# A graph-attention layer and its feed-forward layer on one core: adjacency cast in the transfer, largest score formed by TensorE, one bias product, normalisation on ScalarE

## The reference, cut to what matters

```
xn  = layernorm(x)
seq = (xn @ W_seq).reshape(2048, 16, 32)
score1, score2 = seq . a1, seq . a2                       # per head
scores = leaky_relu(score1[i] + score2[j], 0.2) + (1 - adj) * -65500
hidden = softmax(scores) @ seq  -> (2048, 512) @ W_out + b_out
x = x + elu(hidden)
xn = layernorm(x)
routed = top-2-of-8 experts (latent 256) on xn;  shared = relu(xn @ up.T)**2 @ down.T
x = x + routed + shared
```

## Time and profile before

| | |
|---|---|
| median of 3 runs | 1060.65 us (1060.53 to 1062.79) |
| profiled execution | 1060.79 us, its span 1058.9 us |
| busy: PE, DVE, ACT, POOL | 95%, 76%, 63%, 24% of the span |
| PE's first product with x; first attention unit | 17.82 us; 99.76 us |
| first to last tile of the output projection | 487.86 to 566.77 us |
| mean granted clock of PE | 0.98 of full |

### The profile page before, as it was taken

How to read it: one execution, slowest core, us unless ns; L and a number is a source line. 1 busy time by engine, 2 the same in 40 slices (tenths; PEclk the granted TensorE clock), 3 DMA queues, 4 the chain that set the end, 5 groups by cost and what they waited for, 6 DMA issues and landing times.

```text
span 1058.9 us, 27195 instructions
## 1 busy us (share of the span) xinstructions
PE 1006.7 (95%) x11256; PEld 890.0 (84%) x11256; DVE 803.9 (76%) x1197; ACT 666.5 (63%) x990; POOL 251.5 (24%) x271
## 2 busy tenths in 40 slices
PE   5996889999999999999899999999999999989998
PEld 4875889999999999997677888888888877778887
DVE  6776899999999999993699433448775668975554
ACT  2668999999989889933356333344454546655431
POOL 1103124334333443363331000000065000006500
PEclk9996999999999999999899999999999999999999
DMA  8781111111111111623635000020063124453242
GB/s 301 249 313 40 41 62 43 45 61 42 43 52 52 42 43 52 225 67 132 229 116 208 1 1 1 1 80 1 26 207 117 50 80 131 130 158 112 85 134 99
DMA packets 53778, 102.45 MB, mean 97 GB/s; under 512 B 6161, under 2 KB 26257, under 8 KB 53138
## 3 DMA queue, kind: packets, MB, share of 16 engines
q1 hardware_dynamic: 47666, 82.83, 23.6%
q0 software_dynamic: 3072, 8.39, 2.5%
q10 hardware_dynamic: 2928, 9.57, 2.4%
HBM read 74.69 MB, written 26.08 MB: 95 GB/s over the span
## 4 chain that ended last, share of the span: by engine, by line
PE 47%; issue 2%; DVE 2%; DMA 1%; POOL 1%; ACT 0%; SPq 0%; POOLq 0%; DVEq 0%; ACTq 0%
PE bank L1758 16%; PE bank L1291 16%; PE bank L668 3%; PE bank L1835 2%; PE bank L1786 1%; PE bank L1787 1%; PE bank L1789 1%; DMA xs<-sorted_latent_rows 1%; PE bank L1805 1%; PE bank L1779 1%; PE bank L1743 1%; PE bank L1741 1%; PE bank L665 1%; PE bank L1740 1%; DVE acc_rest L1492 0%
## 5 line engine op out<-in xcount | busy, mean ns | idle before, releaser
L730 ACT ACTIVATE arena<-arena 128x1024 fp8e4<-128x1024 f32 x320 | 336.6, 1136 | 2.5 <-ACT arena L722 1.6
L956 PE MATMUL bank<-arena 128*128 128x132 f16 x4096 | 285.6, 222 | 19.0 <-DVE arena L816 7.6
L956 PEld LDWEIGHTS bank<-arena 128*128 128x128 fp8e4 x4096 | 246.6, 98 | 20.8 <-issue 8.6
L1291 PE MATMUL bank<-xt,up_parts 128*128 128x512 f32 x768 | 186.2, 391 | 0.0
L1758 PE MATMUL bank<-down_parts,h_parts 128*128 128x512 f32 x768 | 184.5, 389 | 0.1
L960 PE MATMUL bank<-arena 128*128 128x66 f16 x4096 | 173.5, 196 | 0.0
L794 DVE TENSOR_SCALAR arena<-arena 128x1024 uint8<-128x1024 f32 x192 | 167.8, 940 | 2.7 <-DMA arena<-s_rows 2.7
L1758 PEld LDWEIGHTS bank<-down_parts,h_parts 128*128 128x128 f32 x768 | 143.9, 188 | 30.5 <-issue 0.5
L1291 PEld LDWEIGHTS bank<-xt,up_parts 128*128 128x128 f32 x768 | 142.3, 188 | 28.6 <-ACT relu_sb L1240 0.2
L960 PEld LDWEIGHTS bank<-arena 128*128 128x128 fp8e4 x4096 | 154.9, 98 | 0.0
L1265 DVE TENSOR_TENSOR relu_sb<-relu_sb 128x512 f32<-128x512 f32 x64 | 44.4, 693 | 118.0 <-ACT relu_sb L1240 110.9
(11 more groups left out here) (231 smaller groups left out, 1403.9 us busy)
## 6 DMA issues: line engine op xcount, KB each, us to landing
hid<-in_adjT SPq DMA_DIRECT2D x32, 512.0 KB, 5.8
arena<-s_rows SPq DMA_DIRECT2D x30, 512.0 KB, 3.7
sorted_latent_rows<-zeros SPq DMA_DIRECT2D x1, 4992.0 KB, 18.5
xs<-sorted_latent_rows SPq DMA_DIRECT2D x39, 128.0 KB, 2.1
sorted_expert_rows<-expert_y SPq DMA_DIRECT2D x39, 128.0 KB, 1.7
arena<-in_x SPq DMA_DIRECT2D x4, 1024.0 KB, 10.8
xr<-in_x SPq DMA_DIRECT2D x16, 256.0 KB, 2.8
up_sb<-in_upT ACTq DMA_DIRECT2D x1, 4096.0 KB, 14.0
```

Of the source, the lines that this page charges most:

```text
L730: last = nc.scalar.activation(m8[:, k, j, :], s1b[:, k % 2, :], ACT.Sigmoid, bias=bias_now[:, k % 2, j:j + 1], scale=STEEP, saturate=False)
L956: last = nc.tensor.matmul(o, m8[:, k, j, i * P:(i + 1) * P], vs[:, b, j, :], start=(j == 0), stop=(j == T - 1))
L1291: last = nc.tensor.matmul(bank[6 + s % 2][:, :], sa[:, s % 2, a, k, :], xt[c][:, b, k, :], start=(i == 0), stop=(i == len(mm) - 1))
```

## The change

Setup: GpSimd issues eight transfers of 512 adjacency rows by 1024 columns that cast float32 to fp8 on the way (+1; `apply_empty_rows` now sets the sign as well as the empty rows), after tile 2 and 3 of x have landed and ahead of its roots; the 32 casts on DVE and ACT are gone. Weights are loaded, centred (now on ACT) and transposed by quarters; x in groups of 2, 2, 4, 4, 4 tiles. Constants are issued by ACT. The largest score over the partitions is formed by a transpose and a product on PE with a maximum on DVE, in place of a reduction on GpSimd. Score rows are stored by SP, the first two ahead of the others. The values of the first head are made in two parts (12 tiles, 4 tiles), and the first unit starts on the first part; the order of the first units is changed on all engines.

Output projection: the bias as one product with 128 rows instead of two with one; the second layer norm as one ACT instruction with scale and bias, for which GpSimd forms -mean/std in two further steps; up is loaded in four parts, issued after tiles 2, 4, 6 and 8, down after tile 10.

The diff, cut to its core (left out: buffer placements, semaphore names, ACT's order in setup, which loses its casts, and the sign constants):

```diff
...
+        TOP_BANK = bank[4]
+        X_GROUPS = ((0, 2), (2, 4), (4, 8), (8, 12), (12, 16))
+        def x_group(t):
+            return next(g for g, (a, b) in enumerate(X_GROUPS) if a <= t < b)
         def setup_loads(sp):
-            sp.dma_start(ident, ident_in[:, :]).then_inc(consts_loaded, 16)
-            sp.dma_start(a_cols_sb, a_cols[:, :]).then_inc(consts_loaded, 16)
-            sp.dma_start(a_mask_sb.rearrange("p c h -> p (c h)"), a_mask[:, :]).then_inc(consts_loaded, 16)
-            for c in range(2):
-                sp.dma_start(wt_sb[:, 2 * c:2 * c + 2, :], w_seqT[c * 2 * P:(c + 1) * 2 * P, :].rearrange("(c p) k -> p c k", p=P)
-                             ).then_inc(wt_loaded[c], 16)
-            for g in range(4):
-                sp.dma_start(x_sb[:, 4 * g:4 * g + 4, :],
-                             x[512 * g:512 * g + 512, :].rearrange("(t p) d -> p t d", p=P)
-                             ).then_inc(x_loaded[g], 16)
-            for q in range(HALVES):
-                if q >= AB:
-                    sp.wait_ge(cast_by_act if (q - AB) % 2 else cast_by_dve, (q - AB) // 2 + 1)
-                sp.dma_start(adj_in[:, q % AB, :], adjT[(q % T) * P:(q % T + 1) * P, (q // T) * IC:(q // T + 1) * IC]
-                             ).then_inc(adj_loaded[q % AB], 16)
+            for c in range(KD):
+                sp.dma_start(wt_sb[:, c, :], w_seqT[c * P:(c + 1) * P, :]).then_inc(wt_loaded[c], 16)
+            for g, (a, b) in enumerate(X_GROUPS):
+                sp.dma_start(x_sb[:, a // 8, a % 8:a % 8 + b - a, :], x[a * P:b * P, :].rearrange("(t p) d -> p t d", p=P)).then_inc(x_loaded[g], 16)
+            sp.wait_ge(st_copied, 6)
+            sp.dma_start(s1_dram[0:2, 0:IC], s1_rows[0:2, 0:IC]).then_inc(s1_stored, 16)
+            sp.wait_ge(s1_stored, 16)
+            for k in range(2):
+                sp.dma_start(s1b[:, k, :], s1_dram[k:k + 1, 0:IC].to_broadcast([P, IC])).then_inc(s1_staged[k], 16)
+            sp.wait_ge(st_copied, 8)
+            sp.dma_start(s1_dram[2:H, 0:IC], s1_rows[2:H, 0:IC]).then_inc(s1_stored, 16)
+            sp.dma_start(s1_dram[:, IC:], s1_rows[:, IC:]).then_inc(s1_stored, 16)
+            sp.wait_ge(s1_stored, 48)
...
+            def centre_w(c):
+                act.wait_ge(w_mean_ready, c + 1)
+                nc.scalar.activation(wt_sb[:, c, :], wt_sb[:, c, :], ACT.Identity, bias=w_nmean[:, c:c + 1]).then_inc(w_centred, 1)
+            def high_w(c):
+                act.wait_ge(w_in_psum, c + 1)
+                nc.scalar.copy(w_hi[:, :, c * P:(c + 1) * P],
+                               bank[4 + c][:, :].rearrange("p (k n) -> p k n", k=KD)).then_inc(w_high, 1)
...
+            def load_adjacency(half):
+                cols = slice(half * IC, (half + 1) * IC)
+                for g in range(AG):
+                    pool.dma_start(adj8[:, 4 * g:4 * g + 4, cols],
+                                   adjT[512 * g:512 * g + 512, cols].rearrange("(j p) i -> p j i", p=P)
+                                   ).then_inc(adj_loaded[half], 16)
+            pool.wait_ge(x_loaded[1], 16)
+            load_adjacency(0)
+            load_adjacency(1)
+            root(0)
+            root(1)
             largest(0, slice(H, H + 1))
+            root(2)
+            root(3)
...
+            def mean_w(c):
+                dve.wait_ge(wt_loaded[c], 16)
+                step(nc.vector.bn_stats(w_stat6[:, c, :], wt_sb[:, c, :]))
+                step(nc.vector.bn_aggr(w_mv[:, c, :], w_stat6[:, c, :]))
+                nc.vector.tensor_scalar(w_nmean[:, c:c + 1], w_mv[:, c, 0:1], -1.0, None, ALU.mult).then_inc(w_mean_ready, 1)
+            def low_w(c):
+                dve.wait_ge(w_high, c + 1)
+                part = w_hi[:, :, c * P:(c + 1) * P]
+                nc.vector.tensor_tensor(w_lo[:, :, c * P:(c + 1) * P], bank[4 + c][:, :].rearrange("p (k n) -> p k n", k=KD),
+                                        part.bitcast(f32), ALU.subtract).then_inc(w_ready, 1)
...
+                dve.wait_ge(s_in_psum, 2)
+                step(nc.vector.reduce_max(topm[0:H, :], TOP_BANK[0:H, 0:P], AX.X))
+                nc.vector.tensor_scalar(topd[0:H, :], ident[0:H, 0:H], topm[0:H, 0:1], None, ALU.mult).then_inc(tops_ready, 1)
+                dve.wait_ge(s_in_psum, 3)
+                step(nc.vector.tensor_copy(topr[:, 0:H], TOP_BANK[:, P:P + H]))
...
+            bound_v()
+            row_stats(0, 1)
+            for c in range(KD):
+                low_w(c)
             low_x(0, 1)
+            row_stats(2, 3)
+            low_x(2, 3)
+            variances(0)
             stats(1)
-            low_x(2, 3)
             low_wa()
-            cast(0)
+            low_x(4, 5, 6)
             stats(2)
-            low_x(4, 5, 6)
-            cast(2)
+            low_x(7, 8, 9, 10)
             stats(3)
-            cast(4)
-            low_x(7, 8, 9)
-            bound_v()
-            cast(6)
-            low_x(10, 11, 12)
-            cast(8)
-            low_x(13, 14, 15)
-            cast(10)
+            low_x(11, 12, 13, 14, 15)
             bound_factor()
-            cast(12, 14)
             any_neighbour(0)
             natural_scores()
-            cast(16, 18)
             exponents()
-            cast(20)
-            apply_empty_rows((0,))
-            cast(22)
-            apply_empty_rows((1,))
-            cast(24)
+            any_neighbour(1)
+            apply_empty_rows((0, 1))
             scale_columns()
...
+            def largest_scores():
+                pe.wait_ge(tops_ready, 2)
+                pe.wait_ge(st_copied, 5)
+                nc.tensor.transpose(TOP_BANK[0:H, 0:P], tops[:, 0:H], ident).then_inc(s_in_psum, 1)
+            def spread_largest():
+                pe.wait_ge(ones_ready, 1)
+                pe.wait_ge(tops_ready, 3)
+                nc.tensor.matmul(TOP_BANK[:, P:P + H], ones_h[0:H, :], topd[0:H, :], start=True, stop=True).then_inc(s_in_psum, 1)
...
             project(4)
-            transpose(13, 14, 15)
-            scores(2)
+            scores(3)
             project(5)
-            scores(3)
+            scores_to_tokens()
             project(6)
-            scores_to_tokens()
+            scores_to_rows()
+            largest_scores()
             project(7)
-            scores_to_rows()
+            spread_largest()
             degrees(0)
-            project(8, 9, 10, 11, 12, 13, 14, 15)
+            project(8, 9, 10, 11, 12, 13)
             degrees(1)
+            project(14, 15)
...
-            for a in range(2):
-                nc.tensor.matmul(bank[2 + t % 2][:, :], ones_r[0:1, :], bout_parts[0:1, a, :], start=(a == 0), stop=False)
+            nc.tensor.matmul(bank[2 + t % 2][:, :], ones_r, bout_parts, start=True, stop=False)
...
-                cast(27)
-                copy_v(11)
-                cast(29)
                 act.wait_ge(bias_copied, 1)
                 act.wait_ge(s1_staged[0], 16)
-                compare_rows(0, DVE_J, DVE_J + 1)
+                compare_rows(0, DVE_J, DVE_J + 2)
+                copy_v(8)
+                compare_rows(0, DVE_J + 2, DVE_J + 4)
+                copy_v(9)
+                compare_rows(0, DVE_J + 4, DVE_J + 6)
+                copy_v(10)
+                compare_rows(0, DVE_J + 6, DVE_J + 8)
+                copy_v(11)
+                compare_rows(0, DVE_J + 8, T)
                 copy_v(12)
-                compare_rows(0, DVE_J + 1, DVE_J + 2)
-                cast(31)
-                copy_v(13)
-                compare_rows(0, DVE_J + 2, DVE_J + 4)
-                copy_v(14)
-                compare_rows(0, DVE_J + 4, DVE_J + 6)
-                copy_v(15)
-                compare_rows(0, DVE_J + 6, DVE_J + 9)
-                split_high(0, 0)
-                compare_rows(0, DVE_J + 9, T)
                 nc.scalar.copy(bias_now[:, 1, :], step_bias[:, 1, :]).then_inc(bias_copied, 1)
                 act.wait_ge(bias_copied, 2)
                 act.wait_ge(s1_staged[1], 16)
-                compare_rows(1, DVE_J, DVE_J + 4)
+                compare_rows(1, DVE_J, DVE_J + 2)
+                copy_v(13)
+                split_first(0, slice(0, T_A))
+                compare_rows(1, DVE_J + 2, DVE_J + 3)
+                copy_v(14)
+                compare_rows(1, DVE_J + 3, DVE_J + 5)
+                copy_v(15)
+                compare_rows(1, DVE_J + 5, DVE_J + 6)
+                split_first(1, slice(T_A, T))
+                compare_rows(1, DVE_J + 6, T)
                 split_high(0, 1)
...
+                def low_first(part, tiles):
+                    dve.wait_ge(hi_copied, part + 1)
+                    nc.vector.tensor_tensor(vs[:, 0, tiles, WD:], vtmp[:, tiles, :], vs[:, 0, tiles, 0:WD],
+                                            ALU.subtract).then_inc(lo_ready, 1)
+                def products_first(tiles):
+                    n = tiles.stop - tiles.start
+                    dve.wait_ge(v_copied, T)
```

(71 more changed lines are left out.)

277 lines of the change are left out of this document (131 added, 146 removed).

## The result

The changed kernel takes 1036.47 us (median of 4 runs, 1034.23 to 1037.96), the kernel before 1060.59 in the runs beside it: a ratio of 0.9766, 95% interval [0.9744, 0.9789]. A second set of five runs gave 0.9778 [0.9750, 0.9805]. The profiled execution has a span of 1035.2 us against 1058.9. The forecast was 1034.2.

A forecast was written before the change was run, and what follows sets the result against it. TensorE, busy 95% of 1058.9 us, was taken to bound the kernel, with VectorE setting attention's pace. 1060.8 - 17.7 (setup and attention) - 8.9 (output projection) = 1034.2 us, range 1023 to 1054.

The forecast's parts named there:

- (b): Setup, first x product to token scores: one projection less, slightly more transposes; token scores at 47.6 us against 54.26.
- (c): Setup, token scores to first compare: PE's largest score costs DVE about 3 us standing; compare at 69.2 us against 74.38.
- (d): Attention, first compare to DVE's collection of the sums: 55.4 us instead of 70.25; collection at 124.6 against 144.63.
- (e): Setup: casting adjacency transfer at 394 GB/s lands at 61 us, asked for at 58.7; setup and attention give -17.7 us.
- (f): Setup: GpSimd's eight transfer issues before its roots cost 1 to 2 us each; root 0 needed near 20 us.
- (g): Output projection: each tile loses a one-row product; products take 3.05 us instead of 3.52, PE alone 4.02 a tile.
- (i): Output projection: no delayed x tile -7.5 us, first elu -1.0, issues in the loop +0.7, tail +1.0; stage sum -8.9.
- (h): Output loop: projection end to hidden tile four ahead takes 9.0 to 9.5 us; 4.3 us a tile, 2.1 us gained.
- A: Rival, 14%: per-row descriptor cost or DVE's work delays GpSimd's issues; root 0 20 us late, setup gives 0: 1052 us.
- B: Rival, 8%: casting adjacency transfer itself slow, second half after 87 us, about 210 GB/s; at 197 GB/s 1070 us.
- C: Rival, 13%: everything at its better end, adjacency in time, 4.05 us output tiles, no tail: 1027 us.
- D: Rival, 15%: output cycle longer through GpSimd contention, or first head's second part late; 4.5 us tiles, setup gains 12: 1043.

The follow-up runs named there:

- experiment 11: Changed kernel with the largest score per head formed by GpSimd's reduction over the partitions again: 1035.71 us, 0.9780 of the kernel before.
- experiment 3: Changed kernel with up weights and the first half of down weights issued at the output projection's start again: 1041.74 us, 0.9839 of the kernel before.
- experiment 7: Changed kernel with GpSimd normalising hidden tile t ahead of the root of tile t-4 instead of behind it: 1030.77 us, 0.9727 of the kernel before.
- Experiment 9: Changed kernel with ScalarE's third up-weights copy ahead of the last two normalisations, the last one behind the first down-weights copy: 1031.53 us, 0.9730 of the kernel before.
- experiment 8: Changed kernel with the hidden tile ahead of the root and GpSimd's multiply waiting for VectorE's second sum of tile t-4: 1027.74 us, 0.9699 of the kernel before.

## Why the prediction was right, and where it was wrong

1034.2 was forecast and 1036.5 measured; the difference of 24.1 us stands against 26.6. The two halves are not equally good: -18.6 for -17.7, and -4.4 for -8.9. That the sum is nevertheless off by only 2.3 us is in part luck: setup brought 0.9 more than forecast, and the later stages, which the sum put at nothing, 0.7.

**Setup and attention.** (a) First product at 12.7 for 13.1. (b) Token scores at 48.9 for 47.6: the first projection ran at about half its rate in this execution, 5.2 us instead of 2.9, which I had not foreseen. (c) First compare at 70.3 for 69.2, 1.1 us late from the same cause; the largest score's cost of 3 us of standing was right (2.52 behind the projection), but set beside a wrong reading of GpSimd's reduction (experiment 11). (d) 55.1 us from compare to collection, 55.4 forecast, and 19.2 us of gain at the collection for 20. Before the collection the trace has one gap of VectorE that ScalarE ends, 0.48 us at 87.81, where the kernel before had 10.05 and 2.51, so ScalarE's lead was all but enough. (e) The adjacency came in time: it lands at 58.0 to 58.7 where a run shows it, against 61 forecast, because the transfer read 428 GB/s and not 394; GpSimd's issues began at 10.05 for 7.8, but the DMA engines had been full since 5 us. The 2.3 us that I took off were not needed. The slow first projection took 1.5 of them back, so that here, too, two errors went against each other. There is no slack in it, though: where the first projection runs at its full rate, VectorE stands before this transfer, and nothing more is to be had ahead of it. (f) The issues cost 0.78 us each, for 1 to 2 forecast, and root 0 came at 21.1 for 20, behind VectorE and not behind the issues.

**Output.** (g) The products of a tile take 3.05 us as forecast. (i) The stall was worth 7.5 us, and its return 4.3 to 7.7 (experiment 3). That no x tile would be delayed was wrong by the 1.04 us of one tile.

The step that failed first is (h). It named the right chain and mis-sized it: 4.49 us a tile for 4.3, which is also what I had named as a sign of being wrong. TensorE waits for the hidden tile from GpSimd in seven of the eleven tiles, 0.30 to 1.38 us. From the end of a projection to the hidden tile four ahead I had 9.0 to 9.5 us; the trace has 9.80 for the tile shown (499.45 to 508.20 + 1.05), 10.57 for the one before it (494.84 to 503.82 + 1.59), and 9.9 in the mean of four in a row. With the 3.5 us back to the end of a projection, 13.45 us for three tiles, this is the 4.48 measured. The moved normalisation puts GpSimd's multiply on one of VectorE's two sums, 0.46 to 0.73 us of the chain. I had looked for contention on GpSimd's small products only (0.19 us each, less than I gave them) and had weighed the shared port for setup's descriptors, where it did nothing, but not for the loop. The loop gave 0.6 us where 2.1 less 0.7 were forecast, the start-up 0.1 for 1.0: 1.7 of the 4.5 us that are missing. (h) also had VectorE as no bound; once the chain was open (experiment 7) its contention made it the bound at 4.385 us.

The other 2.8 us are the tail, in (i): +1.0 forecast, +3.8 found. I had seen that the last norm stands ahead of the third copy of up weights and counted one wait; there are two, of 2.58 and 0.47 us, and after 1.87 us of rest the granted clock fell in this execution, for 1.6 us more. Experiment 9 returned 3.6, those 1.6 among them.

**Rivals.** A did not happen by either of its ways. B neither: 428 GB/s of source bytes is the opposite end. C was wrong for the loop, though its 4.05 us was within reach, since experiment 8 shows 3.86 with one more wait. D's tile of 4.5 us came true, by another contention than the one it named, without its loss in setup.

## What to carry to other kernels

When work moves from one engine to another, redraw not only the chain but also which instructions then run beside each other: here two engines met on operands in SBUF, and the 0.46 us a tile taken off VectorE came back as 0.46 to 0.73. An instruction freed on an engine that waits (one bias product) brings less than it takes off (2.3 to 2.5 us for 0.44 in each of twelve tiles) until the chain that it waits for is open; turning two steps of GpSimd's queue and adding a wait brought 7.1 to 8.4 us, as much as the best of the change's output edits (experiment 3). An in-order queue's tail deserves its own list: what stands behind the last waits is paid in full, and a fall of the clock can come on top. And before a profiled span is compared with another, look for stretches at the lower clock in both: here one such stretch is 1.6 us, as much as some of the edits.
